# A five-layer graph attention kernel: the softmax chain moved from TensorE and VectorE to VectorE alone

## The reference

```python
def _gat_layer(x, src, dst, edge_attr_full, W, att, b, ew, eb):
    edge_emb = edge_attr_full @ ew.T + eb
    xw = x @ W
    xj = xw[src].reshape(-1, H, D) + edge_emb.reshape(-1, H, D)
    xi = xw[dst].reshape(-1, H, D)
    alpha = einsum(xi, att_i) + einsum(xj, att_j)
    alpha = leaky_relu(alpha, 0.2)
    amax = segment_max(alpha, dst)
    ea = exp(alpha - amax[dst])
    alpha = ea / (segment_sum(ea, dst)[dst] + EPS)
    return segment_sum(xj * alpha[..., None], dst).mean(axis=1) + b
```

## Time and profile before

| | |
|---|---|
| median of 3 runs | 3900.87 us (3900.3 to 3903.65) |
| profiled execution, own time | 3890.0 us |
| its span | 3888.2 us |
| PE / DVE / ACT / POOL busy | 69% / 50% / 19% / 56% |
| 1955 gathers on POOL, mean | 970 ns |
| five attention layers | from about 508 us to the end |

### The profile page before, as it was taken

The page is one execution under the profiler, slowest core; times in us unless marked ns, Lnnn a source line. Parts: engine busy times, 40 slices in busy tenths (PEclk is TensorE's granted clock), DMA queues, the critical chain, the costliest instruction groups (busy, mean ns, idle before and its releaser), DMA issues.

```text
span 3888.2 us, 49536 instructions
## 1 busy us (share of the span) xinstructions
PE 2666.7 (69%) x14697; PEld 2103.1 (54%) x14697; DVE 1960.4 (50%) x6598; ACT 736.7 (19%) x3177; POOL 2185.9 (56%) x2359
## 2 busy tenths in 40 slices
PE   7768727777692767769277777927777782777778
PEld 6667715555561655556155555615555561555556
DVE  9966634445462444446244444624454461444446
ACT  0067531111122111112211111221111121111111
POOL 0067556666626666662666666266666626666661
PEclk8555555555586555558655555865555585555558
DMA  3212022222202222220222222022222202222221
GB/s 111 87 58 77 14 62 51 51 51 58 49 21 50 51 51 51 58 48 21 50 51 50 51 58 48 20 53 54 50 52 57 46 25 44 53 50 53 53 46 34
DMA packets 111543, 196.44 MB, mean 51 GB/s; under 512 B 34960, under 2 KB 74682, under 8 KB 111274
## 3 DMA queue, kind: packets, MB, share of 16 engines
q0 software_dynamic: 62560, 130.25, 15.3%
q1 hardware_dynamic: 48714, 63.02, 5.3%
HBM read 181.46 MB, written 11.67 MB: 50 GB/s over the span
## 4 chain that ended last, share of the span: by engine, by line
DVE 36%; PE 21%; another core or an unknown queue 19%; issue 14%; DVEq 5%; ACTq 2%; ACT 2%; POOL 1%; DMA 0%; POOLq 0%; SPq 0%
DVE acc L1214 9%; PE bank L756 7%; PE bank L764 4%; PE bank L758 3%; DVE pw L1178 2%; DVEq L1037 2%; DVE ai_win L1111 2%; DVE alpha L1114 2%; PE bank L701 2%; ACTq L567 2%; DVEq L1214 2%; PE bank L782 2%; DVE ee L1113 1%; DVE ring L878 1%
## 5 line engine op out<-in xcount | busy, mean ns | idle before, releaser
L497 POOL DMA_INDIRECT ring<-table,srci x1955 | 1897.1, 970 | 1018.8 <-issue 533.5
L756 PE MATMUL bank<-pw,ring 128*128 128x48 f32 x3910 | 1205.0, 405 | 265.2 <-DVE pw L1178 208.4
L756 PEld LDWEIGHTS bank<-pw,ring 128*128 128x128 f32 x3910 | 934.4, 294 | 397.2 <-DVE pw L1178 222.5
L1214 DVE TENSOR_TENSOR acc<-acc,bank 128x72 f32 x1955 | 449.9, 230 | 1258.0 <-remote 735.7
L567 ACT COPY ai_win<-ai_rows 128x48 f32 x1955 | 355.9, 229 | 1826.6 <-issue 1736.8
L758 PE MATMUL bank<-onehot,est 128*36 128x24 f32 x3910 | 599.4, 239 | 19.7 <-issue 19.7
L758 PEld LDWEIGHTS bank<-onehot,est 128*36 128x36 f32 x3910 | 368.4, 144 | 194.4 <-issue 28.4
L479 POOL TENSOR_TENSOR ring<-ring,acc 128x512 f32<-128x512 f32 x98 | 130.3, 1333 | 262.0 <-ACT ring L532 258.4
L504 POOL TENSOR_TENSOR S<-S 128x128 f32<-128x128 f32 x125 | 57.4, 459 | 377.9 <-ACT S L579 373.5
L764 PE MATMUL bank<-onehot,identf 128*128 128x504 f32 x320 | 204.5, 759 | 0.0
L701 PE MATMUL bank<-onehot,ring 128*128 128x24 f32 x784 | 173.3, 387 | 42.8 <-DVE acc L1063 33.6
(11 more groups left out here) (203 smaller groups left out, 3070.1 us busy)
## 6 DMA issues: line engine op xcount, KB each, us to landing
ring<-table,srci POOLq DMA_INDIRECT x1955
ai_rows<-lo_dram SPq DMA_DIRECT2D x28, 896.0 KB, 4.4
at<-in_attr SPq DMA_DIRECT2D x65, 224.0 KB
table<-ring SPq DMA_DIRECT2D x15, 390.0 KB, 3.8
table<-ring SPq DMA_DIRECT2D x5, 325.0 KB, 3.4
result<-ring SPq DMA_DIRECT2D x24, 64.0 KB
x_mid<-ring SPq DMA_DIRECT2D x3, 384.0 KB, 2.7
S<-in_dst_flat SPq DMA_DIRECT2D x6, 182.0 KB
```

What stands on the lines that cost most here:

```text
L497: nc.gpsimd.indirect_dma_start(out=ring[:, slot(t), :], out_offset=None, in_=table, in_offset=bass.IndirectOffsetOnAxis(ap=srci[:, t:t + 1 ...
L756: nc.tensor.matmul(o[:, 0:H * WIN], ring[:, slot(t), 0:D], pw[:, g % 3, k, :, :].rearrange("p h w -> p (h w)"), start=True, stop=True)
L1214: V.tensor_tensor(win, win, grp_sum(g, k).rearrange("p (r w) -> p r w", r=REG), ALU.add)\
```

## The change

The chain has no product on TensorE any more. Edges stand in blocks of 32 partitions (`QB`, `NQB` = 4), and VectorE's transposition of 32x32 blocks turns `alpha`, [128, 2 x 32], so that each partition holds 32 successive edges of a tile for each head. DVE scans these 64 values in both directions, collects the ends of all 4 x 28 pieces on the two partitions of the heads by a second transposition and four copies, scans those 112 values, spreads the carries by four copies and a third transposition, and merges them by a maximum with the flags of the piece (`first_add`, `last_add`). The exponentials of chunk and rescaling are one instruction on ACT over 66 columns. `rescale` takes its factor from `dd` with two small DVE instructions. The orders change too: `windows_sum` of chunk c+1 stands after groups 0, 1 and 2, ahead of the addition of groups 1, 2 and 3; `chain_alpha` is part of `chain_scan`; ACT does `windows(c+1)` after `exps(c)`; `keep_warm` is left only between the groups of the last three chunks (11 instead of 32 per layer). In the preamble the rows of destinations are loaded in 36 DMAs instead of 18 and POOL clears their buffer first.

```diff
             def exps(layer, c):
-                gc, hk = layer * NC + c, H * CH[c]
-                act.wait_ge(diff_phi, gc + 1)
-                nc.scalar.activation(phi[:, 1, :], phi[:, 0, :], ACT.Exp).then_inc(exp_phi, 1)
+                gc = layer * NC + c
                 act.wait_ge(diff_al, gc + 1)
-                nc.scalar.activation(bwd[0:hk, :], bwd[0:hk, :], ACT.Exp).then_inc(exp_al, 1)
+                nc.scalar.activation(dd[:, 0:H * QB + H], dd[:, 0:H * QB + H], ACT.Exp).then_inc(exp_al, 1)
...
                 windows(layer, 0)
-                windows(layer, 1)
-                exps(layer, 0)
-                for c in range(NC - 1):
-                    if c + 2 < NC:
-                        windows(layer, c + 2)
-                    exps(layer, c + 1)
+                for c in range(NC):
+                    exps(layer, c)
+                    if c + 1 < NC:
+                        windows(layer, c + 1)
...
-                        if c == NC - 4 and i == lag(c):
-                            keep_warm(6)
-                        elif c >= NC - 3 or c == NC - 4 and i > lag(c):
+                        if c >= NC - 3 and i + 1 < len(GC[c]):
                             keep_warm(1)
-                        if more and i == lag(c):
-                            chain_alpha(layer, c + 1)
-                        if more and i == lag(c) + 1:
-                            chain_rows(layer, c + 1)
-                        if more and i == lag(c) + 2:
-                            chain_cols(layer, c + 1)
-                    if more:
-                        if c >= NC - 4:
-                            keep_warm(1)
-                        chain_probs(layer, c + 1)
-                        if c >= NC - 4:
-                            keep_warm(2)
...
+                link(V.scalar_tensor_tensor(out=alpha[:, :, :], in0=alpha[:, :, :], scalar=SLOPE, in1=alpha[:, :, :],
+                                            op0=ALU.mult, op1=ALU.max))
+                link(V.transpose(aT[:, :, :], alpha[:, :, :]))
+                aTf, fwdf, bwdf = (b[:, :, :].rearrange("p h e -> p (h e)") for b in (aT, fwd, bwd))
+                st, en = (b[:, c, :, :].rearrange("p h e -> p (h e)") for b in (start_add, end_addR))
+                V.tensor_tensor_scan(fwdf, st, aTf, -BIG, ALU.add, ALU.max)
+                V.tensor_tensor_scan(bwdf[:, ::-1], en, aTf[:, ::-1], -BIG, ALU.add, ALU.max)
+                V.tensor_copy(ends[:, 2, 0:H], first_add[:, c, QB - 1:QB].broadcast_to((P, H)))
+                link(V.tensor_copy(ends[:, 3, 0:H], last_add[:, c, 0:1].broadcast_to((P, H))))
+                V.tensor_copy(ends[:, 0, 0:H], fwd[:, :, QB - 1])
+                link(V.tensor_copy(ends[:, 1, 0:H], bwd[:, :, 0]))
+                link(V.transpose(endsT[:, :, :], ends[:, :, :]))
+                link(V.tensor_tensor(fwd[:, :, :], fwd[:, :, :], bwd[:, :, :], ALU.max))
+
+            def chain_rows(layer, c):
+                k = CH[c]
+                r = NQB * k
+                for i in range(NQB):
+                    V.tensor_copy(seq[:, :, i:r:NQB], endsT[i * QB:i * QB + H, :, 0:k])
...
+                V.tensor_tensor_scan(carry[:, 0, 2:r + 2], seq[:, 2, 0:r], seq[:, 0, 0:r], carry[:, 0, 1:2],
+                                     ALU.add, ALU.max)
+                link(V.tensor_tensor_scan(carry[:, 1, 0:r][:, ::-1], seq[:, 3, 0:r][:, ::-1], seq[:, 1, 0:r][:, ::-1], -BIG,
+                                          ALU.add, ALU.max))
+                link(V.tensor_tensor(cmax[:, :], carry[:, 0, 1:2], carry[:, 1, 0:1], ALU.max))
+                link(V.tensor_scalar(carry[:, 2, 1:P + 1], carry[:, 0, 1:2].broadcast_to((H, P)), cmax[:, :], None,
+                                     ALU.subtract))
+                for i in range(NQB):
+                    ins = V.tensor_copy(into[i * QB:i * QB + H, :, :], carry[:, :, 1 + i:1 + P:NQB])
                 link(ins)
+                link(V.transpose(intoT[:, :, :], into[:, :, :]))
 
             def chain_cols(layer, c):
+                for add, d in ((first_add, 0), (last_add, 1)):
+                    for h in range(H):
+                        ins = V.scalar_tensor_tensor(out=fwd[:, h, :], in0=add[:, c, :], scalar=intoT[:, d, h:h + 1],
+                                                     in1=fwd[:, h, :], op0=ALU.add, op1=ALU.max)
+                    link(ins)
+                V.tensor_copy(dd[:, H * QB:H * QB + H], intoT[:, 2, 0:H])
+                V.tensor_tensor(dd[:, 0:H * QB].rearrange("p (h e) -> p h e", h=H), aT[:, :, :], fwd[:, :, :],
+                                ALU.subtract).then_inc(diff_al, 1)
+                link(V.transpose(maxes[:, :, :], fwd[:, :, :]))
...
+                v.wait_ge(exp_al, gc + 1)
+                link(V.transpose(probs[:, :, :], dd[:, 0:H * QB].rearrange("p (h e) -> p h e", h=H)))
...
                     for i, g in enumerate(GC[c]):
-                        if more and q >= 3 and i < 3:
-                            windows_sum(layer, c + 1, i)
-                        if more and i == q:
-                            chain_alpha(layer, c + 1)
+                        if more and q >= 3 and 1 <= i <= 3:
+                            windows_sum(layer, c + 1, i - 1)
                         add_group(layer, g)
```

More of the change, by code:

```diff
@@ L33 @@
 LAST_BASE = NP - WIN
+QB = 32
+NQB = P // QB
 SLOPE = 0.2
@@ L379, in _ @@
             sp.dma_start(lo_dram, lof).then_inc(lo_w, 16)
-            for hh in range(H):
+            sp.wait_ge(rows_clear, 1)
+            for i in range(NQB):
                 for dst, off in ((rcur, 1), (rprev, 0), (rnext, 2)):
@@ L460, in _ @@
                              base=0, pattern=[[-1, P]], channel_multiplier=1).then_inc(made, 1)
-            GP.memset(sel[:, :, :], 0.0).then_inc(sel_set, 1)
-            pool.wait_ge(sel_set, 1)
-            for h in range(H):
-                GP.memset(sel[:, h, h * FA:(h + 1) * FA], 1.0)
-                GP.memset(sel[:, h, HF + h:HF + h + 1], 1.0).then_inc(sel_set, 1)
+            GP.memset(rows_all, 0.0).then_inc(rows_clear, 1)
             for g in range(GCN_G):
@@ L800, in self_tile @@
                                      Wl[:, layer % 2, :], start=True, stop=True).then_inc(s_ps, 1)
-                chain_alpha(layer, 0)
-                chain_rows(layer, 0)
-                chain_cols(layer, 0)
-                chain_probs(layer, 0)
                 for c in range(NC):
-                    more = c + 1 < NC
                     for i, g in enumerate(GC[c]):
@@ L868, in _ @@
             link(V.tensor_copy(iota_p, iotap_i))
+            for buf in (alpha, ends, carry, into):
+                V.memset(buf[:, :, :], 0.0)
+            link(V.tensor_scalar(phi_mask[:, 0:1], iota_p, float(FA), None, ALU.is_lt))
+            link(V.tensor_scalar(phi_mask[:, 1:2], iota_p, float(HF), None, ALU.is_lt))
+            link(V.tensor_tensor(phi_mask[:, 1:2], phi_mask[:, 1:2], phi_mask[:, 0:1], ALU.subtract))
+            for h in range(H):
+                link(V.tensor_scalar(mask_tmp[:, :], iota_p, float(HF + h), None, ALU.is_equal))
+                link(V.tensor_tensor(phi_mask[:, h:h + 1], phi_mask[:, h:h + 1], mask_tmp[:, :], ALU.add))
             def split_key(key, lo, hi):
@@ L1054, in _ @@
                     window_one_hots(c + 1)
-                if i == 6 and c < 2 * len(ROW_BLOCKS):
+                if i == 6 and c < 4:
                     chunk_flags(c)
@@ L1199, in rescale @@
                 base = window_bases(TC[c], 1)
-                v.wait_ge(phi_ps, layer * NC + c + 1)
+                p0 = H * QB
+                link(V.tensor_scalar(dd[:, p0 + H:p0 + REG], phi_mask[:, 0:1], dd[:, p0:p0 + 1], None, ALU.mult))
+                link(V.scalar_tensor_tensor(out=dd[:, p0 + H:p0 + REG], in0=phi_mask[:, 1:2], scalar=dd[:, p0 + 1:p0 + 2],
+                                            in1=dd[:, p0 + H:p0 + REG], op0=ALU.mult, op1=ALU.add))
                 if c:
@@ L1246, in _ @@
                     q = lag(c)
-                    if more and q < 3:
-                        for part in range(3):
-                            windows_sum(layer, c + 1, part)
                     for i, g in enumerate(GC[c]):
-                        if more and q >= 3 and i < 3:
-                            windows_sum(layer, c + 1, i)
-                        if more and i == q:
-                            chain_alpha(layer, c + 1)
+                        if more and q >= 3 and 1 <= i <= 3:
+                            windows_sum(layer, c + 1, i - 1)
                         add_group(layer, g)
@@ L1259, in _ @@
                             self_rows(s_tile_of(c, i))
+                        if more and q < 3 and i == 0:
+                            for part in range(3):
+                                windows_sum(layer, c + 1, part)
                         if more and i == q:
```

181 lines of the change are left out of this document (59 added, 122 removed).

## The result

The changed kernel takes 3944.03 us (median of 4, 3940.42 to 3944.58) against 3900.59 us before on the same chip: 1.0115 times, 95% interval 1.010 to 1.013. It is **43 us slower**, where 100 us faster was forecast; the time lies inside the range. The profiled execution took 3944.58 us.

The account below looks back on a forecast made before the run. No engine was full; POOL and the chain were taken to form a loop through the ring's slots. Per layer 10 + 15 - 5 = 20 us, for five layers 100, gave 3900.87 - 100 = 3801 us, range 3700 to 3950.

Parts of the forecast that it names:

- (b): Ten full-chunk intervals per layer: each about 1.0 us shorter after the late release, 10 us per layer gained.
- (c): Start of a layer: first exponential after 28 copies instead of 56, at about 1243.2; 15 us per layer gained.
- (d): Last chunks: 7 us saved by dropped products, 9 lost by DVE, a few by the clock; 5 us per layer lost.
- (a): The chain on DVE: about 6.4 us per chunk for about 3.7 before, 2.7 us more DVE work; PE loses products and waits.
- no net change: Rival: gains of full chunks and layer start are waited for elsewhere in the ring; 3895 to 3900 us, chance 0.10.
- a few by the clock: Last chunks: unsized loss of a few us per layer because PE, no longer kept busy, would run at a lower clock.
- (e): Preamble: 18 more loads and a cleared buffer, hidden beside the GCN's loads; costs nothing, some 8 us if uncovered.
- slower rival: ACT's window copies enter the full chunks' loop, deciding from 21 us of copies; about 3971 us, 70 slower, chance 0.26.
- POOL-bound case: Full chunks run at POOL's pace, 35 us (about 3520) or 37 us (about 3620); chance for both 0.12.

Follow-up runs that it names:

- e4b_slack: Changed kernel with ten further transpositions (3 us of DVE) in the chain of each of ten full chunks per layer; first chip, 4004.34 us, 1.0282 to before.
- b_order: Kernel before with the changed kernel's order on ACT alone (exponentials ahead of the next chunk's window copies); first chip, 3895.14 us, 0.9994 to before.
- b_cool: Kernel before with the changed kernel's 11 dense products per layer instead of 32; second chip, 3537.38 us, 1.0309 to before.
- b_pad: Kernel before with 6 words of padding ahead of the GCN's small arrays, nothing else changed; second chip, 3419.64 us, 0.9990 to before.
- b_same: Kernel before, unchanged, run on the second chip; 3417.97 us.
- a_same: Changed kernel, unchanged, run on the second chip; 3508.25 us, 1.0244 to before.
- e1_warm: Changed kernel with all 32 dense products per layer of the kernel before, at the same places; second chip, 3504.74 us, 1.0245 to before.

## Why the prediction was wrong

In the prediction's own terms, us per layer in the profiled executions:

| | forecast | measured |
|---|---|---|
| (b) ten full-chunk intervals (exponential 1 to 11) | 10 gained | 3.0 lost |
| (c) start of a layer (first gather to exponential 1) | 15 gained | 2.0 gained |
| (d) last chunks (exponential 11 to 14) | 5 lost | 11.2 lost |

So 26 of the 32 us per layer between forecast and result are gains that did not come, and 6 are the tail. The first part made the forecast wrong; without the tail's 56 us the time would have stayed where it was.

**(a) The chain's price.** The kinds were right, the sum short. DVE rose from 187.36 to 230.54 us in 400, where 215 was forecast: 4.4 us per chunk, not 2.7. Transpositions measured 0.24 to 0.31 (0.30 taken). The mis-sized term is the rows, 2.9 us forecast and 4.3 measured (687.90 to 692.22), and in it the copies on two partitions: eight of them, of 96 and 112 columns, take 0.28 to 0.31 us each, 2.4 us per chunk; I took the smallest instruction's 0.146. By e4b_slack, where 3.3 us of chain lengthened the interval by 0.9, the 1.7 us are worth some 0.5 us per chunk, an estimate.

**(b) Full chunks: the step that failed.** I laid groups 4 to 6 behind the late release of group 3 with 0.6 us of waiting each. The trace of before already had a second late release: the addition at 828.30 after 5.72 us idle, beside POOL's resumption:

```profile
828.44 0.95 POOL L497 DMA_INDIRECT ring<-table,srci  x1 [1.90 <-remote]
```

The prediction shows the addition and gives its wait no term, as if it went with the chain's products. The changed kernel has no product to wait for and the wait stayed. The "no net change" rival named the mechanism, POOL's pauses, and was right here: the interval of a full chunk went from 40.9 to 41.2 us where 1.0 less was forecast, and in the chunk shown e4b_slack's third pause alone answers to the chain. Why the releases come late was not found.

**(c) Start of a layer.** Two steps failed. The exponential was to run as soon as ACT was free, at about 1243; it ran at 1263.58, since DVE's burst of 37 instructions outlasts the 21 that run at pace beside POOL's uninterrupted issue, and the old one of 23 hardly did. And an early exponential isn't worth what it gains: in b_order it came 24 us earlier, and 4 us were left by chunk 11.

**(d) The tail.** Forecast a loss of 5, measured 11.2 (13.8 on the second chip). The direction and the clock were named, the size was not: "a few by the clock" stood in the sum where b_cool shows 16 us for the products alone. This term turned a result of no change into a slower one.

**(e) The preamble** was to cost nothing and gained 11.8 us, of which b_pad's addresses give 3.2 (on the second chip).

**The rivals.** The slower rival (copies in the loop) did not happen: a chunk's copies took 5 to 11 us behind the start of a layer, below its 21, and chunks stayed at 41.2. Only chunk 1 of layer 0 had 24.5 us of them, and its exponential came 58.7 us after chunk 0's. Slower was right for another reason. The POOL-bound case, 35 to 37 us per chunk, is what the second chip shows for both kernels. There DVE's work does seem to reach POOL: a gather's mean goes from 977 ns in b_same to 989 in a_same, 0.3 us in 28 gathers, and that is what a full chunk grows by (exponential 1 to 11, 35.9 to 36.2 us each). On the first chip it went from 970 to 973. The Trainium skill, page "SBUF — State Buffer", section "Who interferes with whom", says that of VectorE in a two-port mode and GpSimd the one that issues first shuts the other out for its whole instruction; the second chip's longer gathers agree in kind, but which of the added instructions does it no run shows.

## What to carry to other kernels

Before taking products off TensorE, look at where they stand: in a stretch that needs the full clock, dense products seem to count by their place as well as by their number, and a change that moves the work around them can undo them. A kernel with and without the products, both before and after the change, tells the clock's loss from the change's own. When an engine waits twice in a period, explain both waits from the releasing side before giving either back. Two late starts that fall on the same instant on two engines probably share a cause that neither engine's own work will move.

## What the runs showed of the hardware

- The same program takes 12% less on one kind of chip or condition than on the other (3419 and 3901 us), all of it in the stretches in which POOL issues gathers.
- On the slower one, while POOL issues indirect DMAs without a pause, ACT and DVE stand idle 1.1 to 2.6 us before many of their small instructions, after a burst of 21 at pace on DVE; with POOL silent for 15.2 us all 37 of the burst run at pace, and the 28 copies right behind it take 4.84 us instead of 28.4.
- The granted clock falls from 1.00 to 0.50 with PE busy (b_same, 1565.87) as well as idle (e1_warm, 1582.46), and in e1_warm it stayed at 0.50 for 34 us in which PE was busy without a pause on groups with single dense products between them.
- On the second chip a gather's mean is 977 ns in b_same and 989 in a_same, with more small instructions on DVE.
- An addition of 128x512 on POOL takes 1334 or 1185 ns by the addresses of its operands alone.
- A copy of 2 partitions x 96 takes DVE 0.31 us, as long as a transposition of 128x128 (0.31).
